# Adjacency row products: three products of the last contraction block stacked into one, the last row tile as 32 columns in four column groups, and bias rows hi and lo in one product

## What is computed

```python
# layer 0
deg = adj.sum(axis=1, keepdims=True) + 1.0
out = concatenate([x, adj @ x / deg], -1) @ W.T
# layer 1: three products with the normalised matrix, one after the other
A = adj * dinv[:, None] * dinv[None, :]
n1 = layernorm(relu(A @ h1) + h1)          # h1 = x @ W1 + b1
n2 = layernorm(relu(A @ h2) + n1)          # h2 = n1 @ W2 + b2
n3 = layernorm(relu(A @ h3) + n2)          # h3 = n2 @ W3 + b3
# layer 2: the entries of tanh(adj * adj) above zero, at most 700 in a row
h2 = tanh(h @ W_proj + b_proj)
feat = relu(new_adj @ (h2 @ W_gcn) + b_gcn)
# layer 3: attention with four heads over adj, then shared and expert layers
```

## Time and profile before

| | us |
|---|---|
| median of three timed runs | 2302.53 (2302.17 to 2304.77) |
| span of the profiled execution | 2300.6 |
| TensorE busy in it | 1991.3 (87%) |
| VectorE busy | 1567.9 (68%) |
| ScalarE busy | 1097.9 (48%) |
| L1037, L1038, L1039 together, the products of `three` (2420 of each) | 1982.4 summed, overlapping |
| mean granted TensorE clock | 0.942 of full |

### The profile page before, as it was taken

How to read it: one execution, slowest core, us unless ns; L and a number is a source line. 1 busy time by engine, 2 the same in 40 slices (tenths; PEclk the granted TensorE clock), 3 DMA queues, 4 the chain that set the end, 5 groups by cost and what they waited for, 6 DMA issues and landing times.

```text
span 2300.6 us, 42794 instructions
## 1 busy us (share of the span) xinstructions
PE 1991.3 (87%) x16187; PEld 1354.2 (59%) x16187; DVE 1567.9 (68%) x3124; ACT 1097.9 (48%) x2149; POOL 449.8 (20%) x455
## 2 busy tenths in 40 slices
PE   6999286999999999939995799759967999999788
PEld 3887263678888888827763588647754222222333
DVE  6766665654455468765668799545567999999565
ACT  7454275522222235417764678336555224242655
POOL 0000474100000013217761100157620000000000
PEclk9999697999999999969997899879988999999899
DMA  7999367556565679765756477333232432322000
GB/s 206 328 354 322 122 154 162 210 211 235 216 227 223 237 265 403 290 220 168 235 181 176 101 194 196 134 122 94 84 111 70 122 117 86 90 83 91 1 17 33
DMA packets 236975, 396.26 MB, mean 172 GB/s; under 512 B 20640, under 2 KB 189217, under 8 KB 220514
## 3 DMA queue, kind: packets, MB, share of 16 engines
q1 hardware_dynamic: 211974, 340.97, 44.7%
q0 software_dynamic: 15296, 43.88, 7.2%
q10 hardware_dynamic: 9504, 8.65, 1.2%
HBM read 309.88 MB, written 83.56 MB: 171 GB/s over the span
## 4 chain that ended last, share of the span: by engine, by line
PE 58%; DVE 22%; DMA 8%; ACT 5%; issue 4%; POOL 2%; SPq 1%; ACTq 0%; DVEq 0%; POOLq 0%
PE ps L1037 9%; PE ps L1039 9%; PE ps L1038 9%; DVE BIG L2683 7%; PE ps L273 4%; PE ps L274 4%; PE ps L275 4%; PE ps L2184 4%; PE ps L2505 4%; DMA BIG<-in_adjT 3%; PE ps L2186 2%; PE ps L2511 2%; DMA X<-rows_split,idxg 2%; PE ps L2160 1%; DVE BIG L2678 1%
## 5 line engine op out<-in xcount | busy, mean ns | idle before, releaser
L1037 PE MATMUL ps<-R,BIG 128*128 128x256 f16 (+1 forms) x1936 | 530.8, 274 | 10.3 <-DVE BIG L1609 5.9
L1039 PE MATMUL ps<-R,BIG 128*128 128x256 f16 (+1 forms) x1936 | 527.9, 273 | 0.0
L1038 PE MATMUL ps<-R,BIG 128*128 128x256 f16 x1936 | 527.7, 273 | 0.0
L2505 PE MATMUL ps<-BIG 128*64 128x452 f32 x1056 | 230.8, 558 | 24.1 <-DVE BIG L2683 20.4
L1037 PEld LDWEIGHTS ps<-R,BIG 128*128 128x128 f16 x1936 | 187.6, 97 | 43.8 <-issue 13.2
L1038 PEld LDWEIGHTS ps<-R,BIG 128*128 128x128 f16 x1936 | 189.8, 98 | 22.9
L1039 PEld LDWEIGHTS ps<-R,BIG 128*128 128x128 f16 x1936 | 188.0, 97 | 26.0
L2683 DVE SCALAR_TENSOR_TENSOR BIG<-BIG 128x904 f32<-128x904 f32 x176 | 192.4, 1155 | 1.6
L2567 ACT ACTIVATE BIG<-X,BIG 128x64 f32<-128x64 f32 x264 | 70.2, 337 | 233.0 <-PE ps L2511 233.0
L2505 PEld LDWEIGHTS ps<-BIG 128*64 128x64 f32 x1056 | 64.3, 136 | 186.7 <-issue 131.2
L2184 PE MATMUL ps<-BIG,X 128*128 x464 | 157.2, 385 | 9.6 <-DVE X L2243 9.6
(11 more groups left out here) (393 smaller groups left out, 4494.1 us busy)
## 6 DMA issues: line engine op xcount, KB each, us to landing
BIG<-adj_split SPq DMA_DIRECT2D x66, 1408.0 KB, 6.3
BIG<-in_adjT SPq DMA_DIRECT2D x42, 1408.0 KB, 11.7
adj_split<-BIG SPq DMA_DIRECT2D x22, 1408.0 KB, 9.8
BIG<-in_adj SPq DMA_DIRECT2D x22, 1408.0 KB, 10.3
BIG<-in_adjT SPq DMA_DIRECT2D x66, 452.0 KB, 3.3
XX<-in_f SPq DMA_DIRECT2D x70, 256.0 KB, 7.7
experts_split<-XX SPq DMA_DIRECT2D x64, 256.0 KB, 4.4
BIG<-experts_split SPq DMA_DIRECT2D x16, 1024.0 KB, 12.9
```

What stands on the lines that cost most here:

```text
L1037: pe.matmul(out[:, 0:n], pr[:, 0, k, :], h[:, k, 0:n], start=start, stop=False)
L1038: pe.matmul(out[:, 0:D], pr[:, 0, k, :], l[:, k, 0:D], start=False, stop=False)
L1039: return pe.matmul(out[:, 0:n], pr[:, 1, k, :], h[:, k, 0:n], start=False, stop=stop)
L2505: pe.matmul(ps[rs, 2 * (h // 2) + c, 0:CW], self.G[:, u, h * HF:(h + 1) * HF], self.PT[:, u, h, cs], start=start, stop=stop)
```

## The change

Three things are changed in the five passes, and one beside them.

1. **The last contraction block** has 20 rows that are not zero. Its three products are put above one another in one matmul: partitions 0 to 31 hold high and high, 32 to 63 high and low, 64 to 95 low and high. `stack_high` (ScalarE, a copy of 20 partitions) and `stack_low` (VectorE, a difference on 20 partitions) fill the matrix side, `last_rows` the feature side. `three` is one matmul for k = 21.
2. **The last row tile** is 32 columns wide instead of 128. `short_tile` spreads its 64 products over four column groups, which write partitions 0, 32, 64 and 96 of one bank; ScalarE copies the four partial sums out (`parts_out`), and one float32 matmul with `fold` adds them (`fold_parts`), inside the next tile. The tile is moved from position 21 to position 11 (`AT`, `ORDER`). The turns, linear products and logits near it get new places.
3. **Bias rows**: high and low part lie on partitions 0 and 32 of one tensor (`rowhl`, `bghl`), with zeros between them, and one matmul with 64 rows of ones adds both.
4. The constants of this are made on VectorE at the start, and `ones16` is no longer loaded.

```diff
+SHORT = 32
+BLOCKS = 2 * KT - 1
+AT = 11
+ORDER = [*range(AT), KT - 1, *range(AT, KT - 1)]
...
+        def last_rows(v, h, src, scale=None):
+
+            hi, lo = h[0:LAST, KT - 1, 0:D], h[32:32 + LAST, KT - 1, 0:D]
+            if scale is None:
+                v.tensor_tensor(lo, src[0:LAST], hi, ALU.subtract)
+            else:
+                v.scalar_tensor_tensor(lo, src[0:LAST], scale[0:LAST], hi, ALU.mult, ALU.subtract)
+            return v.tensor_copy(h[64:64 + LAST, KT - 1, 0:D], hi)
...
         def three(pe, out, pr, k, h, l, n, start, stop):
 
+            if k == KT - 1:
+                return pe.matmul(out[:, 0:n], pr[:, 0, k, :], h[:, k, 0:n], start=start, stop=stop)
...
+        def short_tile(pe, s, bank, pr, h, l, n):
+
+            for q in range(3 * KT - 2):
+                g = slice(32 * (q % 4), 32 * (q % 4) + 32)
+                first, end = q < 4, q >= 3 * KT - 6
+                if q < KT:
+                    mm = pe.matmul(ps[g, bank, 0:n], pr[:, 0, q, :], h[:, q, 0:n], start=first, stop=end)
+                elif q < BLOCKS:
+                    mm = pe.matmul(ps[g, bank, 0:n], pr[:, 1, q - KT, :], h[:, q - KT, 0:n], start=first, stop=end)
+                else:
+                    mm = pe.matmul(ps[g, bank, 0:D], pr[:, 0, q - BLOCKS, :], l[:, q - BLOCKS, 0:D], start=first, stop=end)
+            mm.then_inc(s["qp"], 1)
+
+        def parts_out(act, s, bank, n, count):
+            s.wait(act, "qp", count)
+            act.activation(parts[:, 0:n], ps[:, bank, 0:n], ACT.Copy).then_inc(s["qs"], 1)
+
+        def fold_parts(pe, s, out, n, count, stop=True):
+            s.wait(pe, "qs", count)
+            return pe.matmul(out, fold[:, :], parts[:, 0:n], start=True, stop=stop)
+
+        def stack_high(act, s, pr, a):
+
+            act.wait_ge(ac.sem, ac.n)
+            act.activation(pr[32:32 + LAST, 0, KT - 1, :], a[0:LAST, KT - 1, :], ACT.Copy).then_inc(s["hi"], 1)
+
+        def stack_low(v, pr, a):
+
+            return v.tensor_tensor(pr[64:64 + LAST, 0, KT - 1, :], a[0:LAST, KT - 1, :], pr[0:LAST, 0, KT - 1, :], ALU.subtract)
...
@@ P0: the store, TensorE, the split @@
-                    sp.dma_start(scratch[t], pslot(t % 4)).then_inc(s[f"w{t % 4}"], 16)
+                    o = ORDER[t]
+                    sp.dma_start(scratch[o][:, 0:BLOCKS * wide(o)], pflat(t % 4, o, BLOCKS)).then_inc(s[f"w{t % 4}"], 16)
...
+                    if t == AT:
+                        rows.turn(pe, s, t - 2, 0)
+                        short_tile(pe, s, t % 2, pr, HAh, HAl, D + 1)
+                        rows.logits(pe, s, t - 2)
+                        continue
...
-                        if t >= 2 and k == 4:
+                        if t == AT + 1 and k == 9:
+                            fold_parts(pe, s, ps[:, 4, 0:D + 1], D + 1, 1).then_inc(s["used"], 1)
+                        if t >= 2 and k == (13 if t == AT + 1 else 4):
                             rows.turn(pe, s, t - 2, 0)
...
-                    act.activation(pslot(t % 4)[:, 0], aslot(4 + t % 3), ACT.Copy).then_inc(s["hi"], 1)
+                    pr, a = pslot(t % 4, ORDER[t]), aslot(4 + t % 3, ORDER[t])
+                    ac.inc(act.activation(pr[:, 0], a, ACT.Copy))
+                    stack_high(act, s, pr, a)
...
@@ P1: bias, places of turns and linear products, the short tile and its fold @@
-                    pe.matmul(out, ones16[:, 0:P], rowh[:, a:a + n], start=False, stop=False)
-                    pe.matmul(out, ones16[:, 0:P], rowl[:, a:a + n], start=False, stop=True).then_inc(s["mm"], 1)
+                    pe.matmul(out, ones16[:, 0:P], rowhl[:, a:a + n], start=False, stop=True).then_inc(s["mm"], 1)
...
+                def turn_at(m):
+
+                    if m < 2:
+                        return ((2, 12), (3, 6))[m]
+                    late, k = {AT - 2: (1, 14), AT - 1: (2, 9), AT: (2, 6), AT + 1: (1, 21)}.get(m % KT, (1, 16))
+                    return m + late, k
+
+                def linear_at(m):
+
+                    if m < 2:
+                        return ((3, 2), (3, 14))[m]
+                    late, k = {AT - 2: (1, 20), AT - 1: (2, 15), AT: (2, 12), AT + 1: (2, 4), KT - 1: (1, 20)}.get(m % KT, (2, 2))
+                    return m + late, k
...
+                    if t == AT:
+                        if p == 2:
+                            rows.turn(pe, s, t - 3, 2 * KT)
+                        short_tile(pe, s, n % 2, pr, h, l, D)
+                        if p == 2:
+                            rows.logits(pe, s, t - 3)
+                        continue
...
+                        if t == AT + 1 and k == 4:
+                            fold_parts(pe, s, ps[:, (n - 1) % 2, D:2 * D], D, p + 1).then_inc(s["used"], 1)
...
@@ P1, ScalarE's third product @@
                     if t < KT:
                         s.wait(act, "ag", 2 * KT + 2 * t + 1)
                         root_act(act, 4 + t % 4, 1, s)
+                    if t == AT - 1:
+                        parts_out(act, s, (2 * KT + AT) % 2, D, 3)
...
@@ P2: TensorE @@
+                    if t == AT:
+                        rows.turn(pe, s, t - 3, 0)
+                        short_tile(pe, s, t % 2, pr, HAh, HAl, D)
+                        rows.logits(pe, s, t - 3)
+                        continue
...
+                        if t == AT + 1 and k == 10:
+                            last = ps[:, AT % 2, D:2 * D]
+                            fold_parts(pe, s, last, D, 1, stop=False)
+                            pe.matmul(last, ones16[:, 0:P], bghl[:, :], start=False, stop=True).then_inc(s["used"], 1)
...
-                    pe.matmul(out[:, 0:D], ones16[:, 0:P], bgh[:, :], start=False, stop=False)
-                    pe.matmul(out[:, 0:D], ones16[:, 0:P], bgl[:, :], start=False, stop=True).then_inc(s["used"], 1)
+                    pe.matmul(out[:, 0:D], ones16[:, 0:P], bghl[:, :], start=False, stop=True).then_inc(s["used"], 1)
...
@@ the tail @@
-                        pe.matmul(out, rowh[:, a:a + P], ones16[:, 0:CW], start=False, stop=False)
-                        pe.matmul(out, rowl[:, a:a + P], ones16[:, 0:CW], start=False, stop=False)
+                        pe.matmul(out, rowhl[:, a:a + P], ones16[:, 0:CW], start=False, stop=False)
```

252 lines of the change are left out of this document (147 added, 105 removed).

## The result

The changed kernel takes 2291.7 us in the median (2290.5 to 2293.6), the kernel before on the same chip 2303.65. The ratio is 0.9938, 95% interval 0.9926 to 0.9950. The forecast was 2261.0, range 2250 to 2276: the direction came out, but 12 us were gained in place of 41.

What follows compares the result with a forecast made beforehand. TensorE was taken to bound P1, transfers P0 until its last loads, TensorE and VectorE nearly level P2. Gains 28 (P1), 6 (P0), 6 (P2), 2 (tail), -0.5 (start) make 41.5: span 2259.1, timed 2261 us, range 2250 to 2276.

Steps and rivals of the forecast that it cites:

- The fold's 0.65: Short tile's fold, one f32 product of 256 columns: two passes about 0.45 plus 0.2 for changes of form; bounds 0.4, 1.2.
- rivals 1 and 2: Short tile's quartets: 1, weight loads leave gaps, 2266 us, chance 0.12; 2, no overlap at 256 f16 columns, 2277 us, 0.07.
- rival 1: Weight loads show ahead of each short-tile quartet, 0.11 us each, 1.8 per tile; kernel 2266 us, chance 0.12.
- What TensorE saves here reaches the end: P1: TensorE is the bound in its products, so its savings there count in full; P1 gains 28 us.
- the prediction's signs of being wrong: Quartet records one by one 0.11 apart, P1's granted clock below 1.00, or tiles behind the short one waiting over a us.
- so it stays at 8.0 a tile: P2: VectorE's split loses 0.14 us and gains about 0.2, staying at 8.0 while TensorE would need 7.7.
- the short tile takes 4.5 us off it: P2: two VectorE operations of 3.08 us run on a quarter of the width, saving 4.5 of the 6 us forecast.
- The bound for P2: P2's gain, taken as 6 us, lies between 1.3 and 11, the latter if TensorE alone decided.
- the landing of the last full load: P0: position 21's load lands at about 210 us, last eviction 231.4, 6.8 less; gain taken as 6, bounds 0 and 9.
- the -1.7 for the smaller stores: P0: stores 1/44 smaller bring the last full load 1.7 us earlier; the short tile's load and store add 2.5.
- Rival 3: P0 and P2 give nothing, transfers and VectorE staying the bound to their ends: 12 us lost, 2273 us, chance 0.13.
- Rival 4: Granted clock falls to 1.2 GHz behind TensorE's new pauses and stays there; kernel slower, 2309 us, chance 0.04.

## Why the prediction was right and wrong

- **Stacked block, bias rows and short tile in P1's products 1 and 2: right.** 8.20 a tile in place of 8.53, the short tile 1.87 for 2.0, the fold 0.43 for 0.65; 20.6 came of 21.7. That the whole kernel got faster rests on these two products. The fold's 0.65 was worked out loosely: a step of 0.48 for 452 columns makes 0.54 for two of 256, not 0.45. Missing is a wait of 1.6 at the turn of product 2 beside a count, three tiles behind the short one; with the counts at other tiles it is gone (176.6).
- **The overlap and rivals 1 and 2.** 64 products of 0.11 in 1.87 us are 3.8 side by side: the 16 quartets start 0.11 apart, the four of one within about 0.01. The trace does not agree with the 3.07 of the Trainium skill (TensorE: Matmul & The Clock Gate, Part 3), by which the tile would have taken an estimated 2.3; that figure is measured there on four row tiles with a contraction of 32 and 512 columns, not on column groups, which the prediction did not say. The loads of L1088 take 92 to 97 ns for 32 columns, no less than those of 128, as rival 1 said, but no gap shows: the quartets follow one another at the rate of full products. What the Trainium skill (TensorEngine Tiling (Array Packing), Feature Incompatibilities) says of the fast weight load under column tiling has no price in this trace. Rivals 1 and 2 fall.
- **P1's product 3: the wait behind the short tile was right, what stands around it was not.** The step that failed is "P1 is bound by TensorE" with "What TensorE saves here reaches the end", applied to the third product, for which only "137.46 of 137.91" was looked at; its DMA share of 0.88 is a mean over the whole product, and the seven counts on VectorE had no term there. In the changed kernel it is 1.01 from 845 to 900 and 0.79 on both sides, and the trace of before, cut finer, had shown it:

```profile
861.00:920.00 59.00, 58.64 (x587) 51.59 (x585) 47.93 (x131) 30.28 (x77) 18.71 (x16) 1.00 1.03 401
```

  TensorE was still busy 58.64 of 59.00 beside a DMA share of 1.03: two limits level with each other, so the 4.6 of the stacking and the short tile's gain ran into loads and counts. Predicted 6, measured 1.6; with the counts and their loads elsewhere it is 7.5 (163.1 - 155.6). Two of the prediction's signs of being wrong came here: a granted clock of 0.97 (845 to 900), and waits of 1.21 and 2.14 in tiles behind the short one.
- **P2: the sign was wrong, -9.8 for +6.** Two steps failed. VectorE "gains an operation on 20 partitions (about 0.2), so it stays at 8.0 a tile": the copy took 0.28, ScalarE's copy ahead of it 0.31, for which P2 had no term, and the cycle became 8.26 (8.02 before). Taken out: 6.3 to 6.9. And "the short tile takes 4.5 us off it": it does, but in the rounds in which its data are prepared, four and two tiles ahead of its matmuls. TensorE's 5 us are saved when VectorE has full rounds for the tiles behind. They hand over once a tile, which is the likely reason that neither gets ahead to use both; the runs show only that the same tile costs 3.5 at the twelfth place and gives 6.8 at the last. The fold behind a waiting turn then made them wait for each other: 3.4 to 4.2. The bound for P2 went from 1.3 to 11 and left out a loss, and it was a loss that came.
- **P0: 3.4 for 6 in this execution.** The step that failed is the landing of the last full load: 210 predicted, 214.0 measured, of which 1.8 came with the later start. The rest is not the copies: in the three kernels that have them and no short tile ahead of the last full load, that load lands 144.8 to 145.0 behind P0's first product, as before (144.8). So the -1.7 for the smaller stores did not come, or the copies ate it, and the short tile ahead of the load costs 3.3 (148.1 in the changed kernel) where the sum had +2.5. Behind the landing 7.3 were gained (22.6 to the last result, 29.9 before) of the 7.9 in the sum. The kernels with the same P0 code have 341.3 to 344.0 from P0's first product to P1's first tile (344.7 before), so the stretch gained 1 to 3.
- **Start: -1.8 for -0.5.** The changed kernel and the twelve of the experiments, whose start is the same code, reach P0's first product between 64.3 and 65.9; so it is -0.2 to -1.8, most of it a matter of the execution.
- **Between P1 and P2: -3.4 for 0, and not the change's.** See the last section.
- **Tail: 0 for 2.** The twelve matmuls went, but from P2's last tile to the end it takes what it took. The sum left 0.4 of their 2.4 to TensorE's waits there, and nothing of the 2.4 shows; the cause stays open.
- **Rival 3** (P0 and P2 give nothing) was nearest in mechanism: VectorE's and ScalarE's round set P2's cycle, though not to its end (its late tiles have TensorE busy 47.07 of 48.62), and P0 gave 1 to 3. Its time, 2273, still had all of P1's 28 in it, and a loss in P2 was in no rival. **Rival 4** (the clock) had the right place, stalls near the short tile, but not the size: P2's stretch around it shows 0.91, and P1's product 3 lost 1.7 to it.

## What to carry to other kernels

Where two engines hand over once per tile, ask in which round each of them saves. Here a light tile in the middle of a stage cost time (the two saved in different rounds), and paid where the other engine had nothing large left: try the light tile there first. Before counting a saving of an engine that is busy all through a stage, cut the stage finer and look for a window in which the transfers stand at 1.0 or another engine has work in some tiles only; moving the counts with their loads to emptier products here gave 7.1 us in P1. A small operation has a price to be set against the saving: here 0.28 and 0.31 on two engines against 0.22 on a third. What follows a wait on an engine's queue (a fold behind a turn) inherits the wait, and hands it on.

## What the runs showed of the hardware

The stretch from P1's last tile to P2's first has the same code, but for some small operations at its end, in the changed kernel and the twelve of the experiments. Its length was 314.2 to 319.2 in their profiled executions, and it goes with the granted clock: the five executions up to 316.1 spent 84.6 to 88.6 us of it at the lower level (1.2 GHz), the eight from 316.6 on 91.6 to 95.4. Two of them by stretch, the changed kernel and the one with no short tile in P2:

```profile
958.00:1269.00 311.00, 221.80 (x1765) 163.97 (x1765) 199.20 (x439) 172.23 (x297) 141.84 (x143) 0.85 0.59 181
```

```profile
959.00:1265.00 306.00, 220.51 (x1765) 163.43 (x1765) 199.08 (x438) 171.99 (x295) 141.05 (x143) 0.86 0.59 184
```

The engines do the same work, 221 and 220 us of it on TensorE; at a granted clock of 0.85 the stretch takes 5 us more than at 0.86. Matmuls of 256 columns start 0.21 apart at the lower level (894 to 897) and 0.11 at the full one, so the 3.4 us more that the changed kernel spends there (92.0 for 88.6) account for 1.7 of the 5 at most; the rest is open, and so is what makes the clock fall in one execution and not in another. A change of 4 us in one stage can be hidden or doubled by stages that it doesn't touch: the 10.9 us of the profiled executions were 26.0 of gains in P0 and P1, 9.8 of a loss in P2, and 5.4 lost in stretches that the edits hardly touch.
